# Attention's float32 products as transpositions, products last in steps without y, aligned tile buffers, and z of the first two chunks in the quantising pass

## What is computed

```python
# layer 0, over all samples together: im is (256, 32*M)
im = relu(x); mn = mean(im, axis=1); im = im - mn
p = clip(u.T @ im, -cv, cv)
q = round((p - min(p)) * 255 / (max(p) - min(p))) ...   # 8 bits, a scale per row
x = u @ q - mean(u @ q) + mn
# layer 1, per sample
out = relu(bn(w_conv1 @ x))                 # 256 -> 256
d = relu(bn(w_dr @ out + b_dr))             # 256 -> 128
cov = (d - mean(d)) @ (d - mean(d)).T / M   # 128 x 128
r = rowsums(w_row * bn(cov)) + b_row        # 4 numbers per channel
att = sigmoid(w_fc @ r + b_fc)              # 256 numbers
return x * att
```

## Time and profile before

| | |
|---|---|
| median of 3 runs | 1867.75 us (1865.58 to 1868.95) |
| profiled execution | 1868.28 us, span 1866.5 us |
| PE busy | 1695.2 us (91%) |
| DVE busy | 1576.0 us (84%) |
| ACT busy | 1475.6 us (79%) |
| mean granted TensorE clock | 0.954 of 2.4 GHz |

### The profile page before, as it was taken

The page is one execution under the profiler, slowest core; times in us unless marked ns, Lnnn a source line. Parts: engine busy times, 40 slices in busy tenths (PEclk is TensorE's granted clock), DMA queues, the critical chain, the costliest instruction groups (busy, mean ns, idle before and its releaser), DMA issues.

```text
span 1866.5 us, 40162 instructions
## 1 busy us (share of the span) xinstructions
PE 1695.2 (91%) x13394; PEld 1317.1 (71%) x13394; DVE 1576.0 (84%) x2897; ACT 1475.6 (79%) x2244; POOL 460.2 (25%) x136
## 2 busy tenths in 40 slices
PE   8999999999993235588899999999999999999999
PEld 8999999999992011366566666666666766666665
DVE  6888888888887788689988888888888888888886
ACT  7777777777778997788778878788788787888886
POOL 7888888888880000000000000000000000000000
PEclk9999999999996567699999999999999999999999
DMA  9998998998999999405546546455465464554535
GB/s 333 375 375 305 375 370 305 378 365 313 373 353 388 430 430 429 194 2 201 191 156 235 169 167 227 157 201 193 165 221 175 163 233 162 189 204 166 213 139 208
DMA packets 141135, 477.37 MB, mean 256 GB/s; under 512 B 10656, under 2 KB 33568, under 8 KB 126368
## 3 DMA queue, kind: packets, MB, share of 16 engines
q1 hardware_dynamic: 141088, 476.75, 69.2%
HBM read 284.04 MB, written 192.68 MB: 255 GB/s over the span
## 4 chain that ended last, share of the span: by engine, by line
PE 51%; DVE 4%; ACT 0%; issue 0%; DVEq 0%; ACTq 0%
PE y_ps L1014 16%; PE z_ps L1040 16%; PE d_ps L965 13%; PE cov_ps L947 5%; DVE hl L1181 1%; DVE gg L1203 1%; PE ch_ps L1025 1%; DVE g L1193 0%; DVE p_res L1274 0%; DVE qr L1149 0%; PE ch_ps L978 0%; PE ch_ps L977 0%; DVE q L1156 0%; PE y_ps L994 0%; PE cov_ps L950 0%
## 5 line engine op out<-in xcount | busy, mean ns | idle before, releaser
L299 POOL TENSOR_TENSOR xl<-early,xh 128x1568 fp32r<-128x1568 f32 x128 | 459.3, 3589 | 97.1 <-ACT xh L258 97.1
L1040 PE MATMUL z_ps<-qr,wl 128*128 128x512 f16 (+2 forms) x896 | 314.5, 354 | 0.0
L1040 PE MATMUL z_ps<-qr,wh 128*128 128x512 f16 (+2 forms) x896 | 314.2, 354 | 0.0
L1181 DVE TENSOR_TENSOR hl<-h,hh 128x1024 f16<-128x1024 f32 (+2 forms) x224 | 243.9, 1089 | 74.5 <-ACT hh L1097 74.3
L258 ACT ACTIVATE xh<-early 128x1568 fp32r<-128x1568 f32 x128 | 194.1, 1517 | 139.8 <-PE pp L316 139.7
L965 PE MATMUL d_ps<-vh,hh 128*128 128x128 f16 x1600 | 280.1, 219 | 7.5 <-DVE hl L1181 7.5
L1092 ACT ACTIVATE h<-z_ps,sb_h 128x512 f32<-128x512 f32 (+2 forms) x448 | 264.0, 625 | 23.6 <-PE z_ps L1040 20.5
L965 PE MATMUL d_ps<-vl,hh 128*128 128x128 f16 x1600 | 279.9, 219 | 0.0
L965 PE MATMUL d_ps<-vh,hl 128*128 128x128 f16 x1600 | 279.9, 219 | 0.0
L316 PE MATMUL pp<-xh,uh 128*128 128x392 f32 x1024 | 267.4, 342 | 9.1 <-ACT xh L258 9.1
L1014 PE MATMUL y_ps<-qr,udh 128*128 128x512 f16 (+2 forms) x784 | 274.1, 353 | 0.0
(11 more groups left out here) (198 smaller groups left out, 2999.7 us busy)
## 6 DMA issues: line engine op xcount, KB each, us to landing
early<-in_x_dram SPq DMA_DIRECT2D x128, 784.0 KB, 6.9
out_dram<-p_res SPq DMA_DIRECT2D x30, 3136.0 KB, 10.2
early<-p_scratch SPq DMA_DIRECT2D x42, 1568.0 KB, 12.7
p_res<-p_scratch SPq DMA_DIRECT2D x112, 512.0 KB, 4.4
p_scratch<-early SPq DMA_DIRECT2D x56, 784.0 KB, 7.8
p_scratch<-late SPq DMA_DIRECT2D x56, 784.0 KB, 7.8
p_res<-p_scratch SPq DMA_DIRECT2D x56, 384.0 KB, 3.2
late_tile<-p_scratch SPq DMA_DIRECT2D x13, 1568.0 KB, 12.8
```

What stands on the lines that cost most here:

```text
L299: nc.gpsimd.tensor_tensor(xl[:, k % 2], xs[:, k], xh[:, k % 2].bitcast(F32), ALU.subtract).then_inc(split_done, 1)
L1040: last = nc.tensor.matmul(z_ps[:, m, 0:w], part[:, k, m * P:(m + 1) * P], qr[:, a, k, columns(s)], start=k == 0 and part is wh, stop=k == ...
L1181: nc.vector.tensor_tensor(hl[:, par, :, 0:w], h32[:, par, :, 0:w], hh[:, par, :, 0:w], ALU.subtract).then_inc(h_split, 1)
```

## The change

- `spread` and `logits` use float32 transpositions by TensorE (`nc.tensor.transpose`) for their products. The row sums that the logits' products made are now made by DVE from PSUM (`logit_sb`), and ACT waits for that.
- In phases of existing samples the logits stand at the end of step 3, behind cov, instead of in step 4 behind y. In steps without y, spread and logits stand last on PE.
- DVE's order in steps without y: gg, conversion, g, hl, the attention's sums, scaling. In steps 1 to 3 ACT scales both halves of the kept y.
- z of chunks 0 and 1 of the first sample is made at the end of the quantising pass; in the first phase z runs a step ahead, in two PSUM buffers in turn, and the constant of y is made in step 4.
- Mean, shift and the extremes of 31 samples are worked out beside the last sample of the statistics pass; the chain of small steps behind it is shorter.
- `p_res`, `early` and `late_tile` start at multiples of 256 bytes.

```diff
-        p_res = sb("p_res", [P, RES, K, M])
+        p_res = sb("p_res", [P, RES, K, M], align=LINE)
...
+                act.wait_ge(x_summed, 1)
+                nc.scalar.activation(mn[:], mn[:], ACT.Copy, scale=1.0 / (N * M)).then_inc(mean_done, 1)
...
+                stored_samples(RES - 1)
+                resident_sub(RES - 1, N - 1, 0)
+                dve.wait_ge(psum_read, K * LATEST)
+                nc.vector.tensor_reduce(pmax[:, :, N * SUBS:], pmax[:, :, 0:LATEST], AX_X, ALU.max)
+                nc.vector.tensor_reduce(pmin[:, :, N * SUBS:], pmin[:, :, 0:LATEST], AX_X, ALU.min)
+                resident_sub(RES - 1, N - 1, 1)
+                dve.wait_ge(relu_done, SUBS * N)
+                nc.vector.tensor_reduce(mn[:], xsum[:], AX_X, ALU.add).then_inc(x_summed, 1)
...
+                for c in range(EARLY_Z):
+                    pe.wait_ge(q_halved, MADE * CH + c + 1)
+                    pe.wait_ge(quantised, TILES * PAIRS - 1 + PARTS if c > 0 else TILES * (PAIRS - 1) + 2)
+                    for m in range(K):
...
+            def z_bank(r2, a, s):
+                return y_ps if first_phase(r2, a) and s % 2 == 1 else z_ps
+            def vector_scales(s):
+                return not 1 <= s <= 3
...
-                        nc.tensor.matmul(ch_ps[:, 0:P], hl_sb[:], ident[:], start=True, stop=True)
-                        nc.tensor.matmul(ch_ps[:, P:2 * P], ones[:], dg[:], start=True,
-                                         stop=True).then_inc(spread_done, 1)
+                        nc.tensor.transpose(ch_ps[:, 0:P], hl_sb[:], ident[:])
+                        nc.tensor.transpose(ch_ps[:, P:2 * P], dg[:], ident[:]).then_inc(spread_done, 1)
...
-                    if s == Y_LAG and exists(r2, a, back=1):
+                    if s == (3 if exists(r2, a) else Y_LAG) and exists(r2, a, back=1):
                         pe.wait_ge(weighted_done, J * n)
+                        wait_from(pe, logits_summed, n - 1)
                         for m in range(K):
-                            last = nc.tensor.matmul(ch_ps[:, 2 * P + m:2 * P + m + 1], weighted[:, m],
-                                                    ones[:, 0:1], start=True, stop=True)
+                            last = nc.tensor.transpose(ch_ps[:, (2 + m) * P:(3 + m) * P], weighted[:, m], ident[:])
                         last.then_inc(logits_done, 1)
...
+                        if has_no_y(r2, a, s):
+                            if s == 1:
+                                covariance(r2, a, s)
+                            reduced(r2, a, s)
+                            if s != 1:
+                                covariance(r2, a, s)
+                            spread(r2, a, s)
+                            logits(r2, a, s)
+                            continue
...
                         reduced(r2, a, s)
                         if s != 1:
                             covariance(r2, a, s)
+                        if exists(r2, a):
+                            logits(r2, a, s)
...
-                            act.wait_ge(logits_done, n)
+                            act.wait_ge(logits_summed, n)
...
-                for c in range(LEAD):
-                    convert(0, c, q_kept(ORDER[0])[:, :, columns(c)])
+                convert(0, LEAD, q_kept(ORDER[0])[:, :, columns(LEAD)])
...
+                    if s == Y_LAG and exists(r2, a, back=1):
+                        dve.wait_ge(logits_done, n)
+                        wait_from(dve, att_done, n - 1)
+                        nc.vector.tensor_reduce(logit_sb[:], ch_ps[:, 2 * P:].rearrange("p (m c) -> p m c", m=K), AX_X,
+                                                ALU.add).then_inc(logits_summed, 1)
...
-                        if s == 1:
+                        if s == 1 or has_no_y(r2, a, s):
                             low_half_of_g(r2, a, s)
...
+                        if not has_no_y(r2, a, s):
+                            sums_of_covariance(r2, a, s)
                         if has_no_y(r2, a, s):
                             rectified_g(r2, a, s)
                             low_half_of_h(r2, a, s)
-                            if has(r2, a, s, CH + Y_LAG):
+                            sums_of_covariance(r2, a, s)
+                            if has(r2, a, s, CH + Y_LAG) and vector_scales(s):
```

More of the change, by code:

```diff
@@ L268, in _ @@
                 nc.scalar.activation(grow_sb[:], grow_sb[:], ACT.Copy, scale=BN / M)
-                nc.scalar.activation(ncv[:], cv[:], ACT.Copy, scale=-1.0)
+                for n in range(2):
+                    nc.scalar.activation(cv2[:, n], cv[:], ACT.Copy)
+                    nc.scalar.activation(ncv2[:, n], cv[:], ACT.Copy, scale=-1.0)
                 for j in range(J):
@@ L334, in _ @@
                     sample(i)
+                pe.wait_ge(mean_done, 1)
+                pe.wait_ge(psum_read, K * (N * SUBS - 1))
+                for m in range(K):
+                    for k in range(K):
+                        last = nc.tensor.matmul(shift[:, m:m + 1], u_sb[:, k, m * P:(m + 1) * P],
+                                                mn[:, k:k + 1], start=k == 0, stop=k == K - 1)
+                last.then_inc(shift_done, 1)
             @block.vector
@@ L457, in _ @@
                 last.then_inc(turned, 1)
-                pe.wait_ge(mean_done, 1)
-                for m in range(K):
-                    for k in range(K):
-                        last = nc.tensor.matmul(shift[:, m:m + 1], u_sb[:, k, m * P:(m + 1) * P],
-                                                mn[:, k:k + 1], start=k == 0, stop=k == K - 1)
-                last.then_inc(shift_done, 1)
                 for j in range(J):
@@ L508, in _ @@
                         last.then_inc(y_made, 1)
+                for c in range(EARLY_Z):
+                    pe.wait_ge(q_halved, MADE * CH + c + 1)
+                    pe.wait_ge(quantised, TILES * PAIRS - 1 + PARTS if c > 0 else TILES * (PAIRS - 1) + 2)
+                    for m in range(K):
+                        for k in range(K):
+                            for part_of in (wh, wl):
+                                last = nc.tensor.matmul(
+                                    early_z[c][:, m, 0:widths[c]], part_of[:, k, m * P:(m + 1) * P],
+                                    q16[:, (MADE * CH + c) % 2, k, 0:widths[c]],
+                                    start=k == 0 and part_of is wh, stop=k == K - 1 and part_of is wl)
+                        last.then_inc(z_done, 1)
             @block.scalar
@@ L846, in has_no_y, with scaled_by_vector @@
                 return not has(r2, a, s, CH + Y_LAG) or made(output_chunk(r2, a, s)[0])
+            def vector_scales(s):
+                return not 1 <= s <= 3
+            def scaled_by_vector(chunks):
+                return sum(vector_scales((c + Y_LAG) % CH) for c in range(chunks))
             def kept_y(o, c):
@@ L1126, in phase @@
                             if made(o):
-                                kept = kept_y(o, c)[:, 0]
-                                nc.scalar.activation(kept, kept, ACT.Identity, scale=att_cy[:, 0, 0:1],
-                                                     bias=att_cy[:, 0, 1:2]).then_inc(y_free, K)
+                                own = 1 if vector_scales(s) else K
+                                for m in range(own):
+                                    kept = kept_y(o, c)[:, m]
+                                    last = nc.scalar.activation(kept, kept, ACT.Identity, scale=att_cy[:, m, 0:1],
+                                                                bias=att_cy[:, m, 1:2])
+                                last.then_inc(y_free, K)
                                 continue
```

244 lines of the change are left out of this document (135 added, 109 removed).

## The result

| | before | after |
|---|---|---|
| median | 1868.35 us (4 runs, 1865.58 to 1870.58) | 1893.83 us (4 runs, 1891.72 to 1897.03) |
| profiled execution | 1868.28, span 1866.5 | 1891.72, span 1889.8 |
| PE, DVE, ACT busy | 91%, 84%, 79% | 90%, 84%, 79% |
| mean granted clock | 0.954 | 0.952 |

The account below looks back on a forecast made before the run. DMA bounds quantising, DVE samples without y, PE samples with y. Terms 9 + 10 - 1.8 - 3.5 + 0.4 = +14 on 1868.3, less 0.5, gave 1882, taken as 1881; range 1867 to 1890 for 8 in 10.

Parts of the forecast that it names:

- Together 1.8 + 0.4 + 1.0 + 0.85 = 4.1 us on the chain: Samples without y: DVE idle behind PE's wait, row sum, ACT's sigmoid and att_cy, ACT's gg; 4.1 us in phases 1 to 3.
- +10 us, bounds 0 (both new waits hidden) and +14: Phases 1 to 4, mostly without y: waits less gains of the new order, about +3, +3, +3 and +1.
- order and scaling: Steps without y: sums of step 1 +0.9, earlier gg -0.7 per sample; ACT's scaling -1.3 in phases 2, 3 and 4.
- row sum, with its waits: Step 4 without y: reduction 0.42, ACT's sigmoid and att_cy about 1.0, then 0.85 idle for ACT's gg, per sample.
- PE's wait for `weighted`: Step 3 without y: PE stands until DVE's `weighted`, so DVE idles 1.8 us where 0 to 0.3 were lost.
- Samples with y: Logits at the end of step 3: PE waits 0.53 us for `weighted`; net 0.34 per sample, times 27 = +9 us.
- if the wait vanished, -0.37 x 27 = -10: Samples with y, lower bound: without PE's wait, four transpositions save 0.37 us per sample, 10 us in all.
- rival at 1860: Samples with y: PE doesn't wait for `weighted`, kernel faster, 1853 to 1863, taken as 1860; chance 0.13.
- PE sets the pace: Samples with y before the change: PE busy in all of the 34.1 us, DVE in 29.6.
- Start of quantising: End of statistics pass: fewer dependent steps make the first quantised tile 2.4 us earlier; -1.8 us, bounds 0 and -2.4.
- Early z: z of chunks 0 and 1 ahead of the chunk loop: d starts sooner; net -3.5 us, bounds -1 and -6.
- Tail: Last sample's chain: one more reduction (0.42), less the transpositions; +0.4 us.

Follow-up runs that it names:

- e8: e5 plus the changed kernel's order and ACT scaling in steps without y; float32 products, logits in step 4, no DVE row sum; 1864.42 us.
- e9: e1 plus 9 products that nobody reads, ahead of the cov products of step 5 in samples without y; 1863.91 us.
- e2: Changed kernel plus unread products in samples without y, 14 ahead of the logits of step 3 and 9 ahead of step 5's cov; 1883.67 us.
- e1: Changed kernel with the logits' transpositions put back in step 4 in every phase; 1867.56 us.
- e3: Kernel before with only spread and logits as transpositions at their old places and row sums by DVE; 1873.05 us.
- e6: e5 with the two products of spread as transpositions, logits still float32 products; 1860.92 us.
- e5: Changed kernel with the chunk loop's spread, logits, row sum, order and scaling of before, keeping early parts and aligned buffers; 1865.45 us.
- e4: Changed kernel with its three buffers at multiples of 32 bytes instead of 256; 1896.20 us.

## Why the prediction was wrong

**The step that failed** is "Together 1.8 + 0.4 + 1.0 + 0.85 = 4.1 us on the chain", with "+10 us, bounds 0 (both new waits hidden) and +14": it costs the waits and leaves PE's speed behind them at full. The 20.0 us divide as follows:

| cause | us | from | forecast |
|---|---|---|---|
| order and scaling | -1.25 | e8 against before | about -3 |
| row sum, with its waits | +3.5 | e9 against e8 | (0.4 + 1.0 + 0.85) x 3 to 4 |
| clock behind the pause of step 5 | +3.4 | e1 against e9 | none |
| PE's wait for `weighted` | +9.2 | e2 against e9 | 1.8 x 3 to 4 |
| clock behind that pause | +5.2 | after against e2, 8.6 less the 3.4 | none |

The kernels before, e8, e9 and e2 have a granted clock of 1.00 in this stretch, so the first, second and fourth line are free of it. Together they are 11.4, near the +10. (The prediction's own terms add up to 11.7: its +3 for phase 1 should be +4.3, since the -1.3 of the scaling is not in that phase.) So the waits were right in place and in sum, with errors that nearly cancel. The wait for `weighted` costs 2.3 to 2.5 us per sample where 1.8 was worked out. The row sum costs some 1.1 where 2.25 was, since the wait of 0.87 for ACT's gg, which I gave to it, stands in e8 too, where there is no row sum; it belongs to the new order, which gains 1.25 instead of 3. DVE's timeline of e8:

```profile
847.79 0.55 DVE L1354 TENSOR_SCALAR p_res<-p_res,att_cy 128x512 f32<-128x512 f32 x1 [0.34 <-ACT att_cy L1183]
849.21 0.69 DVE L1274 TENSOR_TENSOR gg<-g,gg 128x512 f16<-128x512 f32 x1 [0.87 <-ACT gg L1155]
```

The clock, 8.6 of the 20.0 us, was no term of the sum at all. I gave the clock of the first phase its due and did not ask it of the new pauses. (That the 8.6 divide between the two pauses in the changed kernel as e1 and e9 divide them is argued, not measured.)

**Samples with y**: right. Wait 0.45 (forecast 0.53), period 34.34 (34.4), +6.9 (+9). But the bound "if the wait vanished, -0.37 x 27 = -10" and with it the rival at 1860 were wrong: e1, e3 and e6 have no such wait and gain at most 0.18 per sample. "PE sets the pace" was true with less than 0.2 us to spare, and I had looked only at PE's and DVE's queues, not at ACT's release of y's buffer.

**Start of quantising**: its first tile is begun at 566.70 instead of 569.39, its last part at 767.85 instead of 770.01, -2.2 (-1.8). **Early z**: -3.1 (-3.5) in that trace, some 1.7 less by e5's runs. **Aligned buffers**: 0, right. **Tail**: +1.7 instead of +0.4; the part up to the last product grew by 0.3, the rest lies behind it. That rest is not tied to the row sum: e2 and e9 have the row sum and as short a rest as before (19.0 us in all); the kernels after, e1, e3 and e4 have 20.4 to 20.8. Why is open.

## What to carry to other kernels

When a change makes TensorE wait, cost the wait and then the work behind it at the lower clock: here 2.1 us of pause were enough to halve the speed of the next 3 us, and the clock raised the loss from 11.4 to 20.0 us. Before counting a saving on the engine that sets the pace, look for the second bound, buffer releases by other engines included; here it lay less than 0.2 us below. A large change is worth taking apart: the same edits without the moved logits, their transpositions and the row sum gain 9.5 us (e10).

## What was not expected of the hardware

Adding 83 products that nobody reads (e2) made the kernel 10.2 us faster by the medians, and the stretch in which they stand 8.6 us shorter, by the granted clock. From the second sample on, single pauses of up to 1.77 us left it at 1.00 in every traced kernel; pauses of 2.08 us (e1) to 4.23 us (after) brought it to 1.2 GHz each time, for about 3 us, and once in e1 for almost 7. Shorter pauses close together can do it too: at the start of the chunk loop after, TensorE stood still for 0.91 and 1.30 us with 1.05 us of work between, and the clock went from 1.00 (772 to 774 us) to 0.50 (775 to 777). Four float32 transpositions per sample did not lower it (1.00 with y), and each took 0.11 us on the path. Two sigmoids took 0.47 us with the logits in SBUF and 0.40 with them in PSUM.
